# Both transposes of a cross-attention and mixture-attention kernel turned to blocks of features, with a new order of all steps

## The reference

```python
# 1: cross attention, 16 heads of 32, keys beyond the context's length masked
x = x + attention(layernorm(x) @ Wq, ctx @ Wk, ctx @ Wv) @ Wo
# 2: self attention over the 512 tokens; each of q, k, v, o is a mixture
h = layernorm(x)                               # "hidden_states"
pooled = h.mean(axis=1)                        # (8, 512)
logits = relu(pooled @ gw1.T + gb1) @ gw2.T + gb2
top_vals, top_idx = top_k(logits, 2); gates = softmax(top_vals)
def svd_moe(x, Wm, U, S, V, b):                # for q, k, v and o
    return x @ Wm.T + sum_k gates[k] * ((x @ V[idx_k].T) * S[idx_k]) @ U[idx_k].T + b
q, k, v = svd_moe(h, q...) * 32**-0.5, svd_moe(h, k...), svd_moe(h, v...)
x = x + svd_moe(softmax(q @ k.T) @ v, o...)
```

## Time and profile before

| | |
|---|---|
| median of three runs | 1428.75 us |
| lowest and highest | 1421.71, 1436.47 us |
| the profiled execution | 1419.3 us |
| its span, first to last instruction | 1417.5 us |
| mean granted TensorE clock | 0.986 of full speed |
| PE (TensorE matmuls) busy | 1381.6 us, 97% |
| DVE (VectorE) busy | 952.0 us, 67% |
| ACT (ScalarE) busy | 861.4 us, 61% |
| POOL (GpSimd) busy | 679.8 us, 48% |

### The profile page before, as it was taken

How to read it: one execution, slowest core, us unless ns; L and a number is a source line. 1 busy time by engine, 2 the same in 40 slices (tenths; PEclk the granted TensorE clock), 3 DMA queues, 4 the chain that set the end, 5 groups by cost and what they waited for, 6 DMA issues and landing times.

```text
span 1417.5 us, 17150 instructions
## 1 busy us (share of the span) xinstructions
PE 1381.6 (97%) x5704; PEld 699.8 (49%) x5704; DVE 952.0 (67%) x1687; ACT 861.4 (61%) x1499; POOL 679.8 (48%) x411
## 2 busy tenths in 40 slices
PE   8998999999999999999999999999999999999987
PEld 5545444545455554554555544555445454444432
DVE  4463567766767677766777677767777577666572
ACT  2426475866478663865568663976548665565652
POOL 2012143555446462546455463555534455465675
PEclk9999999999999999999999999999999999999999
DMA  7533223432524224532334324332245323233210
GB/s 264 132 88 101 60 67 113 124 77 46 144 70 105 75 54 126 138 91 48 76 118 110 76 59 136 104 89 67 54 121 144 76 46 106 56 96 85 82 39 30
DMA packets 78768, 130.81 MB, mean 92 GB/s; under 512 B 26375, under 2 KB 32135, under 8 KB 75608
## 3 DMA queue, kind: packets, MB, share of 16 engines
q1 hardware_dynamic: 74007, 128.55, 33.8%
q10 hardware_dynamic: 4672, 1.17, 0.4%
HBM read 66.08 MB, written 12.21 MB: 55 GB/s over the span
## 4 chain that ended last, share of the span: by engine, by line
PE 87%; ACT 5%; issue 2%; DVE 2%; POOL 2%; DMA 1%; SPq 1%; ACTq 0%; POOLq 0%; DVEq 0%
PE pj L1211 44%; PE scT L1296 8%; PE acc L1325 8%; PE sc L1268 7%; PE sc L1257 3%; PE pj L1241 2%; PE pj L1334 2%; PE scT L1289 2%; PE pj L1313 2%; PE pj L1305 2%; PE pj L1205 2%; ACT xhat L804 1%; PE pj L1196 1%; PE pj L1184 1%; ACT qs L887 1%
## 5 line engine op out<-in xcount | busy, mean ns | idle before, releaser
L919 ACT ACTIVATE probs<-scT 128x512 f32<-128x512 f32 x512 | 289.0, 594 | 300.6 <-PE scT L1296 294.8
L1042 DVE TENSOR_REDUCE negmax<-sc 128x1 f32<-128x512 f32 x512 | 338.2, 684 | 141.5 <-PE sc L1268 140.6
L778 POOL TENSOR_TENSOR probs_sum<-probs_sum,probs 128x1024 f32<-128x1024 f32 x128 | 300.1, 2366 | 56.8 <-ACT probs L919 56.8
L1069 DVE RECIPROCAL inv_sum<-pj 128x128 f32<-128x128 f32 x256 | 225.0, 921 | 57.6 <-PE pj L1334 40.7
L1268 PE MATMUL sc<-ks,qs 96*128 96x512 f32 x512 | 260.5, 541 | 3.1 <-DVE negmax L1042 1.5
L1211 PE MATMUL pj<-XT,Wqk 128*128 128x512 f32 x512 | 257.4, 599 | 0.6 <-DVE Wqk L1134 0.6
L1296 PE MATMUL scT<-qs,ks 99*128 99x512 f32 x512 | 251.8, 519 | 4.0 <-ACT probs L919 2.7
L774 POOL TENSOR_TENSOR probs_sum<-probs 128x1024 f32<-128x1024 f32 x64 | 151.4, 2372 | 171.7 <-ACT probs L919 171.7
L784 POOL TENSOR_TENSOR uv_stack<-UVS_sb,uv_stack 96x1024 fp32r<-96x1024 f32 x32 | 75.7, 2365 | 178.3 <-ACT UVS_sb L826 178.3
L1296 PEld LDWEIGHTS scT<-qs,ks 99*128 99x128 f32 x512 | 95.1, 191 | 118.4 <-ACT probs L919 59.0
L1268 PEld LDWEIGHTS sc<-ks,qs 96*128 96x128 f32 x512 | 97.5, 192 | 94.9 <-issue 49.7
(11 more groups left out here) (103 smaller groups left out, 1704.9 us busy)
## 6 DMA issues: line engine op xcount, KB each, us to landing
Wqk<-in_WmT SPq DMA_DIRECT2D x16, 1024.0 KB, 6.9
Wvo<-in_WmT SPq DMA_DIRECT2D x16, 1024.0 KB, 6.5
UVS_sb<-in_UVS SPq DMA_DIRECT2D x64, 192.8 KB, 3.4
qs<-stage_lo SPq DMA_DIRECT2D x136, 64.0 KB, 2.0
qs<-qs SPq DMA_DIRECT2D x34, 256.0 KB, 3.1
X<-in_x SPq DMA_DIRECT2D x8, 1024.0 KB, 5.9
ks<-stage_lo SPq DMA_DIRECT2D x128, 64.0 KB, 2.0
ks<-ks SPq DMA_DIRECT2D x32, 256.0 KB, 3.0
```

What stands on the lines that cost most here:

```text
L778: nc.gpsimd.tensor_tensor(probs_sum[:, pair], probs_sum[:, pair], probs[:, kt % 2, pair], ALU.add)\
L919: nc.scalar.activation(probs[:, kt % 2, jj, :], scT[:, ST[step], :], ACT.Exp, scale=SCALE)\
L1042: nc.vector.tensor_reduce(negmax[:, 0, n:n + 1], sc[:, SC[step], :], AX.X, ALU.max, negate=True)\
L1069: nc.vector.reciprocal(inv_sum[:, INV[use], at], pj[:, PJ[left_in(full)], at])\
```

## The change

Three things change. First, a transpose step now makes one block of 128 features of all four token tiles (`xpose(b, half, c)`) and no longer all four blocks of one token tile (`xpose(b, half, t)`). The 128x128 transposes are the same sixteen for each half, but the four that share a bank now need all four normed tiles, and ScalarE's copy fills one row `XT[:, c, :]` of the result from end to end. `q1` waits for the block that it reads, and no longer for all. Second, the token sums go from each block's row straight into `pooled`, and the reduction over the four tiles' partial sums (`tile_sums`, L1097) is gone. Third, the times of nearly all steps in `CALENDAR` and `OWN` are other numbers; the `warm` places, the period and the code of the other steps are as before.

```diff
 CALENDAR = {
-    "normalize": (-1775, 138),
-    "xpose": (-1734, -1732, -1712, -1710, 141, 141, 163, 163),
+    "normalize": (-1958, 33),
+    "xpose": (-1922, -1920, -1896, -1866, 49, 49, 55, 55),
...
-    "token_sums": (145, 157, 163, 166),
-    "gate_hidden": (218,),
-    "gate_top": (235,),
-    "gate_scale": (349,),
+    "token_sums": (50, 53, 56, 57),
+    "gate_hidden": (66,),
+    "gate_top": (70,),
+    "gate_scale": (140,),
...
     if kind == "token_sums":
-        return {"gate_step": 2 if step[2] == TT - 1 else 1}
+        return {"gate_step": 1}
...
-        tile_sums = sb("tile_sums", [P, DC, TT])
...
-            def xpose(step, b, half, t):
+            def xpose(step, b, half, c):
                 if half == 0:
                     act.wait_ge("pj_full", max(act.after("pj_full", "qk", b - 2, DC - 1, w, DC - 1) for w in range(2)))
                 act.wait_ge("pj_full", act.after("pj_full", *step))
-                nc.scalar.activation(XT[:, b % 2, :, t * P:(t + 1) * P],
-                                     pj[:, PJ[step], :].rearrange("p (c n) -> p c n", c=DC), ACT.Copy)\
+                nc.scalar.activation(XT[:, b % 2, c, :], pj[:, PJ[step], :], ACT.Copy)\
                     .then_inc(sems["pj_left_by_act"], 1)
...
-            def token_sums(step, b, t):
-                dve.wait_ge("pj_left_by_act", dve.after("pj_left_by_act", "xpose", b, 1, t))
-                nc.vector.tensor_reduce(tile_sums[:, :, t:t + 1], XT[:, b % 2, :, t * P:(t + 1) * P], AX.X, ALU.add)\
+            def token_sums(step, b, c):
+                dve.wait_ge("pj_left_by_act", dve.after("pj_left_by_act", "xpose", b, 1, c))
+                nc.vector.tensor_reduce(pooled[:, c:c + 1], XT[:, b % 2, c, :], AX.X, ALU.add)\
                     .then_inc(sems["gate_step"], 1)
-                if t == TT - 1:
-                    dve.wait_ge("gate_step", dve.after("gate_step", *step, k=1))
-                    nc.vector.tensor_reduce(pooled[:], tile_sums[:], AX.X, ALU.add).then_inc(sems["gate_step"], 1)
...
-            def xpose(step, b, half, t):
+            def xpose(step, b, half, c):
                 pe.wait_ge("consts_loaded", 64)
                 p = opened(step)
-                pe.wait_ge("xhat_done", pe.after("xhat_done", "normalize", b, half, k=t + 1))
-                for dc in range(DC):
-                    mm = nc.tensor.transpose(pj[:, p, dc * P:(dc + 1) * P], xhat[:, t, dc * P:(dc + 1) * P], ident_sb[:])
+                for t in range(TT):
+                    pe.wait_ge("xhat_done", pe.after("xhat_done", "normalize", b, half, k=t + 1))
+                    mm = nc.tensor.transpose(pj[:, p, t * P:(t + 1) * P], xhat[:, t, c * P:(c + 1) * P], ident_sb[:])
                 mm.then_inc(sems["pj_full"], 1)
...
             def q1(step, b, i, dc):
                 pe.wait_ge("wq1_loaded", 16)
-                pe.wait_ge("pj_left_by_act", pe.after("pj_left_by_act", "xpose", b, 0, TT - 1))
+                pe.wait_ge("pj_left_by_act", pe.after("pj_left_by_act", "xpose", b, 0, dc))
```

More of the change, by code:

```diff
@@ L76 @@
[L76 to L82, removed]
@@ new lines @@
+    "q1_split": (-1802, -1496, -918, -681),
+    "q1_rows": (-1792, -1136, -906, -472),
+    "q1_stack": (-1684, -1111, -701, -377),
+    "pick": (112,),
+    "uv_load": (129, 257, 331, 2776),
+    "csc": (-1466, -1410, -1403, -1348, -1058, -1057, -1032, -1032, -693, -688, -674, -667, -294, -293, -231, -227),
+    "cross_shift": (-1341, -1014, -657, -202),
+    "cross_shift_move": (-1291, -1010, -656, -106),
+    "csT": (-1180, -1179, -1171, -1160, -945, -944, -932, -924, -613, -551, -481, -479, -100, -79, -72, -65),
@@ new lines @@
+    "cpv": (-1112, -676, -467, -55),
+    "cacc": (-1095, -658, -455, -46),
+    "cden": (-990, -634, -467, -56),
+    "cinv": (-987, -979, -955, -936, -541, -529, -491, -489, -466, -463, -447, -361, -55, -55, -32, -29),
+    "wm_load": (62, 217, 471, 3094),
+    "cdivide": (-628, -441, -188, -46, -36, -31, -27),
+    "out1": (-68, -62, -51, -35, -41, -38, -32, -18, -22, -20, -20, -14, -16, -12, -11, -4),
+    "residual1": (-19, -14, -2, -2),
+    "residual_bias": (404,),
+    "token_sums": (50, 53, 56, 57),
@@ new lines @@
+    "gate_hidden": (66,),
+    "gate_top": (70,),
+    "gate_scale": (140,),
+    "uv_hi": (177, 518, 669, 2988),
+    "uv_lo": (224, 558, 736, 3077),
+    "weff": (410, 419, 482, 499, 573, 615, 635, 668, 763, 800, 813, 876, 3239, 3293, 3345, 3382),
+    "qk": (500, 511, 525, 535, 686, 686, 691, 698, 1006, 1077, 1098, 1123, 1126, 1166, 1223, 1238, 1372, 1383, 1383,
+        1406, 1550, 1560, 1561, 1587, 2051, 2076, 2083, 2090, 2093, 2110, 2113, 2120),
+    "qk_split": (556, 700, 1204, 1266, 1407, 1590, 2094, 2133),
@@ new lines @@
+    "qk_rows": (926, 787, 1282, 1295, 1758, 1757, 2123, 2168),
+    "qk_stack": (937, 888, 1336, 1347, 1793, 1790, 2174, 2220),
+    "v": (833, 844, 882, 892, 858, 864, 888, 896, 893, 898, 914, 947, 947, 953, 955, 960),
+    "v_bias": (901, 922, 974, 1008),
[4 rows of a table added]
+    "shift": (1345, 1937, 2172, 2893),
+    "shift_move": (1359, 1976, 2185, 2921),
[5 rows of a table added]
+    "psum": (1550, 1597, 1656, 1752, 1788, 1874, 2075, 2076, 2092, 2098, 2156, 2176, 2561, 2638, 2703, 2803, 2876,
+        2947, 3117, 3218, 3276, 3300, 3347, 3349),
@@ L185 @@
-    "token_sums": {(0, 0): 150, (0, 1): 153, (0, 2): 156, (0, 3): 156, (7, 0): 14403, (7, 1): 14410, (7, 2): 14417,
-        (7, 3): 14420},
-    "gate_hidden": {(0,): 247, (7,): 14443},
-    "gate_top": {(0,): 271, (7,): 14468},
-    "gate_scale": {(0,): 328, (7,): 14515},
-    "pick": {(0,): 301, (7,): 14553},
+    "context_keys": {(0, 0): -13599, (1, 0): -13255, (2, 0): -11180, (3, 0): -10175, (0, 1): -9872, (1, 1): -9570,
+        (2, 1): -3595, (3, 1): -2966},
+    "split_keys": {(0,): -9855, (1,): -2589},
@@ new lines @@
+    "context_values": {(0,): -9750, (1,): -2550, (2,): 0, (3,): 2, (4,): 279},
+    "context": {(0,): -7966},
+    "context_v": {(0,): -3703, (7,): 12559},
+    "wm_load": {(7, 3): 20191, (0, 0): -1471, (0, 1): 315, (0, 2): 763, (7, 1): 14451, (7, 0): 14340, (7, 2): 14679},
+    "uv_load": {(7, 3): 17122, (0, 0): 128, (0, 1): 220, (0, 2): 488, (7, 2): 14624, (7, 0): 14357, (7, 1): 14571},
+    "uv_hi": {(7, 3): 19879, (0, 0): 226, (0, 1): 437, (0, 2): 588, (7, 1): 14754, (7, 2): 14873, (7, 0): 14402},
@@ new lines @@
+    "uv_lo": {(7, 3): 20195, (0, 0): 249, (0, 1): 479, (0, 2): 692, (7, 1): 14798, (7, 2): 14885, (7, 0): 14440},
+    "weff": {(7, 3, 0): 20624, (7, 3, 1): 20709, (7, 3, 2): 20805, (7, 3, 3): 22098, (0, 0, 0): 321, (0, 0, 1): 371,
[12 rows of a table added]
+    "load": {(0,): -16522},
+    "stats": {(0, 0): -11937, (0, 1): -11621, (0, 2): -11416, (0, 3): -10941},
+    "deviation": {(0, 0): -10668, (0, 1): -98, (7, 1): 14261},
+    "normalize": {(0, 0): -9085, (0, 1): -92, (7, 1): 14275},
+    "xpose": {(0, 0, 0): -8945, (0, 0, 1): -8511, (0, 0, 2): -7522, (0, 0, 3): -3857, (0, 1, 0): 6, (0, 1, 1): 21,
[10 rows of a table added]
@@ L191 @@
+    "token_sums": {(0, 0): 8, (0, 1): 21, (0, 2): 23, (0, 3): 46, (7, 0): 14293, (7, 1): 14294, (7, 2): 14295,
+        (7, 3): 14296},
+    "gate_hidden": {(0,): 74, (7,): 14302},
+    "gate_top": {(0,): 101, (7,): 14308},
+    "gate_scale": {(0,): 219, (7,): 14320},
+    "pick": {(0,): 118, (7,): 14345},
     "warm": {(0, 2): -989, (1, 3): -909, (2, 1): -663, (3, 4): -423, (4, 5): 71, (5, 2): 170, (6, 3): 244,
         (7, 3): 323, (8, 2): 334, (9, 3): 555, (10, 4): 768},
-    "residual_bias": {(7,): 16702},
[7 rows of a table removed]
@@ new lines @@
+    "qk_stack": {(7, 0, 0): 15097, (7, 0, 1): 15191, (7, 1, 0): 16629, (7, 1, 1): 16837, (7, 2, 0): 19517,
[4 rows of a table added]
+    "v_bias": {(7, 0): 15138, (7, 1): 15160, (7, 2): 15194, (7, 3): 15312},
[12 rows of a table added]
+    "shift": {(7, 0): 15614, (7, 1): 19706, (7, 2): 21223, (7, 3): 22039},
+    "shift_move": {(7, 0): 16213, (7, 1): 19858, (7, 2): 21325, (7, 3): 22051},
[16 rows of a table added]
+    "psum": {(7, 0, 1, 0): 18221, (7, 0, 1, 1): 18666, (7, 0, 2, 0): 19564, (7, 0, 2, 1): 19641, (7, 0, 3, 0): 19763,
[4 rows of a table added]
+    "accout": {(7, 0): 20198, (7, 1): 21400, (7, 2): 22316, (7, 3): 25822},
@@ L255 @@
+    "mask": {(): -14197},
+    "key_rows": {(0,): -16163, (1,): -5363},
 }
```

122 lines of the change are left out of this document (37 added, 85 removed), and 194 rows, old and new, of tables (CALENDAR, OWN).

## The result

The changed kernel takes **1458.83 us** (median of 3 runs, 1454.54 to 1466.05), the kernel before 1428.75: a ratio of 1.0228, 95% interval 1.0177 to 1.0279. A repeat gave 1460.82 us and 1.0244 (1.0205 to 1.0282). My 1429 us, and the range up to 1443, were too low.

A forecast was written before the change was run, and what follows sets the result against it. TensorE, busy 1381.6 of 1417.5 us, was taken as the bound. Terms of -0.2 - 0.9 + 3.2 - 1.6 + 0 = +0.5 us on the 1428.75 us median gave 1429 us, range 1413 to 1443.

The forecast's parts named there:

- Place 1: From gate_hidden to gate_top, TensorE waits 0.8 us in each of six middle periods, bounds 0.5 and 1.2 us.
- the chain from gate_top to the first `weff`: In a middle period, tight before and after the change: nothing added, 1 us a period as the bad end.
- The clock rival: At each middle gate, two close waits lower the clock: 10 to 20 us lost, 1439 to 1449 us; chance 0.15.
- the `XT` waits: Before the last two transpose steps of each middle period, TensorE's wait for ScalarE's copy goes: -0.66 us a period.
- `q1`'s: In the first sequence, `q1`'s wait for the last copy goes, as its first product needs block 0 alone: -0.9 us.
- The first transpose of a half: Needs all four normed tiles, up to 2.2 us later; taken as 0 in the middle, uncovered up to 2.2 us a period.
- The copies and sums: ScalarE's 64 copies and VectorE's 32 sums of 512 columns keep their cost; their other form is priced at 0.
- the maxima's transpose: In each middle period, TensorE waits 0.4 us for VectorE's split to free the bank, between 0 and 1.2 us.
- joined products: Steps with V or denominators cost less behind their own kind, 136 groups against 144: -1.6 us, between -1.6 and 0.
- `pooled`: In the first sequence, where TensorE waited 1.05 us for it, the last sum of 0.17 us goes: -0.2 us.
- The ends: First cross attention, first gate and last sequence keep nearly the same order: 0, with -10 and +5 us as bounds.

The follow-up runs named there:

- Experiment 7: Kernel before with GpSimd's norm step of the next sequence one addition later, so an addition runs when `hiddenB` is made: 1426.11 us, ratio 1.0008.
- experiments 6: Also `gate_later`: changed kernel with gate_top moved from 70 to 82 in the middle sequences, 1449.43 us; with the second U,V,S load early too, 1438.46 us.
- experiment 5: Changed kernel with `hiddenB` made on ScalarE and the second U,V,S load early: 1431.24 us, ratio 1.0048 to the kernel before.
- experiment 4: Also `uv_early`: changed kernel with each middle sequence's second U,V,S load ahead of the next context's load and second Wm load: 1448.43 us, ratio 1.0148.
- code_fit: New transpose form in the calendar of before, with transposes and pooled sums moved to where all four `xhat` tiles are there: 1441.55 us, ratio 1.0113.
- experiment 3: Also `hidden_act`: changed kernel with `hiddenB` made by one ScalarE instruction instead of by VectorE: 1452.78 us, ratio 1.0194 to the kernel before.
- experiment 1: The changed code with the whole calendar (CALENDAR and OWN) of the kernel before: 1437.24 us, ratio 1.0081 to the kernel before.
- tuned: Changed kernel with `hiddenB` on ScalarE, second U,V,S load early, gate_top at 71.5 and sequence 1's first cross-query stack earlier: 1437.67 us, ratio 1.0080.

## Why the prediction was wrong, step by step

**Place 1 failed; this is the step.** I had TensorE wait 1.85 - 1.06 = 0.8 us at gate_top, with 1.2 as the upper bound. It waits 1.89 us. The 1.85 us came from the first sequence, where GpSimd was not in an addition and `hiddenB` took 0.28 us. That duration is no constant. The trace of before had it at the last gate, with a GpSimd addition running:

```profile
1226.89 2.36 POOL L778 TENSOR_TENSOR probs_sum<-probs_sum,probs 128x1024 f32<-128x1024 f32 x1
1228.00 1.33 DVE L1101 TENSOR_SCALAR hiddenB<-ident_sb,hidden 128x128 f32<-128x128 f32 x1 [0.42 <-ACT hidden L934]
```

I priced the chain gate_hidden, `hidden`, `hiddenB` and never asked what GpSimd does at that moment in the new order, though I wrote that all three engines "have slack". Experiment 7 shows the clash, experiments 6 and 7 its cover, and experiment 5 against 4 its price with what follows it: 0.0100 of the ratio, 14 us.

**A term was missing: the second U,V,S load.** I followed the chain from gate_top to the first `weff` and put it at nothing. That held: no wait stands there (598.33 to 617.33). I did not follow the load for the second weight, which the calendar moves behind the context's keys on SP's queue, nor what is queued behind its scaling on ScalarE. It cost 8.6 us of waits, and 11 us in experiment 4.

**The clock rival had the mechanism and too little chance.** I gave it 10 to 20 us of lost clock; the middle's busy time grew by 17.9 us, inside that. Its total of 1439 to 1449 us fell short because the idle time beneath was 3.2 us in my sum and 15.6 us here. With 0.54 us left at each gate (experiment 5) the middle ran at 1.00, with a fall behind one gate of six; with 1.89 us at 0.98, behind five. I gave it 0.15, since the six waits of 0.66 us had left the clock alone; with the gate's wait sized rightly it was the likely case. But the case that it describes, 0.8 and 0.4 us within some 7 us, did not act as the 1.01 us at the last gate did: in experiment 5 0.54 and 1.0 us within 8 us, and in `code_fit` 1.2 us at once, left the clock at 1.00 in five and in six sequences. The length of one wait does not decide alone, as experiment 3 shows too (a fall behind 0.54 us, none behind 2.02). The rule of the Trainium skill cited there ("TensorE: Matmul & The Clock Gate", section "A second HAM failure mode: psum-queue depth-cycling"), on short idle times between groups of matmuls, pointed the right way; in the changed kernel's middle, each of the seven falls had a single wait of 1.6 to 2.1 us at its start or just before it.

**Right, or nearly:** the `XT` waits (-3.9 us) and `q1`'s (-0.9) went. The first transpose of a half, which I took as covered in the middle, is: its four short waits, 1.4 us, all lie in the first sequence. The copies and sums that I priced at 0 are so: 0.60 us a copy for 0.59, 0.68 a sum in both. The first transpose, uncovered, costs 0.35 us a wait, 10.5 us in all (experiment 1), under the 2.2 us a period that I had as the bad end. **Wrong but small:** the maxima's transpose waits once in the middle, 0.4 us, and not 0.4 us a period, as TensorE comes to it a gate's wait later; in experiment 3, with the gate faster, it waits 1.0 us in four of the six periods. The 1.6 us for joined products are not seen: with both fixes the middle's busy time is 1.5 us over that of before, which its one fall of the clock (0.57 over 4 us, so 1.7 us) accounts for. `pooled` in the first sequence waits 1.4 us, not 0.9. **The ends,** priced at 0: the start lost 7.8 us, outside my +5, the end gained 1.8.

**Open:** the start. Of its 7.8 us, 5.5 are clock; one wait of 1.7 us for the first cross queries' stack was tried (`tuned`) without a gain. How much clock each fix gives back alone is open too: the profiles show the middle's busy time at 994.4 us with neither, 983.1 (`hidden_act`), 980.8 (`gate_later`) or 986.5 (`uv_early`) with one, and 977.9 with both, while the median clocks of all runs are 0.971, 0.973, 0.976, 0.972 and 0.981; the profiled runs of `hidden_act` and `uv_early` were faster than their medians. What besides a wait's length makes the clock fall isn't shown.

## What to carry to other kernels

- A duration taken from a trace holds for the neighbours that it had. Before a short VectorE instruction between two SBUF operands is put on the path, look at what GpSimd runs at that time in the new order, and price the rest of that instruction.
- When a calendar moves, follow every load on its queue to the engine that waits for it, and from there to what stands behind; with an engine at 97% a late item soon becomes a wait, and here the 15.6 us of added idle time came with 17.9 us more busy time at a lower clock.

## What the runs showed of the hardware that I had not expected

- VectorE's 128x128 `tensor_scalar`, 0.28 us alone, took 0.70 to 1.77 us under one GpSimd addition, ending within 0.1 us of it, and 4.50 us under four short ones in a row: splitting the long instruction shortened the wait in the middle and lengthened it at the end.
- A wait's length alone did not tell whether the clock falls: 1.9 us at the gate brought a fall in five of six places (in the changed kernel and in `uv_early` alike), 0.54 us in one of six and in two of six, and 1.2 us in none of six, nor did one of 2.02 us.
- The same kernel's clock differs from run to run (0.968 to 0.979 in `hidden_act`, 1457.5 to 1442 us), so one profile can show a fix as 11 us better than its median.
